# Four graph layers on one core: the projections of the attention layers done two chunks at a time, side by side, with half of the split operands filled by DMA

## The reference

```
L0: h = x @ W (row 0 set to 0); h2 = mask^T summed h; score = h.a1 + h2.a2; out = leaky(score * sum(h))
L1: h = x @ Wh for 4 heads; scores = h h^T; softmax over the masked row; attn @ h + bh, leaky_relu;
    the 4 heads side by side -> z; h2 = z @ Wo; the same attention once more; leaky_relu, layernorm
L2: h = x @ W; e = leaky(h.a_l + (h.a_r)^T, 0.01); masked softmax; attn @ h
L3: the same with slope 0.2 and the other weights
```

## Time and profile before

| | before |
|---|---|
| runs | 6273.06, 6281.87, 6285.5 us (median 6281.87) |
| profiled execution | 6281.5 us, of which the span from the first to the last instruction is 6279.7 us |
| TensorE matmul busy | 5612.5 us, 89% of the span |
| VectorE, ScalarE, GpSimd busy | 4379.2, 3844.2, 1784.7 us |
| mean granted TensorE clock | 0.956 |
| moved by DMA | 55.36 MB |

### The profile page before, as it was taken

How to read it: one execution, slowest core, us unless ns; L and a number is a source line. 1 busy time by engine, 2 the same in 40 slices (tenths; PEclk the granted TensorE clock), 3 DMA queues, 4 the chain that set the end, 5 groups by cost and what they waited for, 6 DMA issues and landing times.

```text
span 6279.7 us, 163342 instructions
## 1 busy us (share of the span) xinstructions
PE 5612.5 (89%) x52064; PEld 4569.8 (73%) x52064; DVE 4379.2 (70%) x7705; ACT 3844.2 (61%) x5701; POOL 1784.7 (28%) x1659
## 2 busy tenths in 40 slices
PE   7679998998989889998989989898899989899866
PEld 4368777886768777786778867787777867788755
DVE  4856567767776677767777677766777677776765
ACT  1046557666576666667576666767576675766665
POOL 0100015014240424205250242404242052402455
PEclk9889999999999999999999999999999999999988
DMA  4200000000000000000000000000000000000000
GB/s 142 59 11 2 2 5 2 2 2 10 4 2 2 2 12 2 2 2 3 11 2 2 2 10 4 2 2 2 12 2 2 2 3 11 2 2 2 8 1 5
DMA packets 98616, 55.36 MB, mean 9 GB/s; under 512 B 88800, under 2 KB 92128, under 8 KB 97760
## 3 DMA queue, kind: packets, MB, share of 16 engines
q1 hardware_dynamic: 59872, 34.45, 2.0%
q10 hardware_dynamic: 37888, 9.97, 0.7%
HBM read 35.49 MB, written 8.91 MB: 7 GB/s over the span
## 4 chain that ended last, share of the span: by engine, by line
PE 69%; issue 9%; DVE 7%; ACT 5%; DVEq 3%; POOLq 1%; POOL 1%; ACTq 0%; DMA 0%; SPq 0%
PE tp L917 22%; PE po L937 20%; PE pss L905 9%; PE pss L906 9%; DVEq L259 3%; DVE rows L1193 2%; PE px L866 2%; DVE pt L1205 2%; PE px L925 2%; ACT pss L1077 1%; ACT rows L1097 1%; PE px L862 1%; POOLq L259 1%; PE px L880 1%; PE px L872 1%
## 5 line engine op out<-in xcount | busy, mean ns | idle before, releaser
L917 PE MATMUL tp<-ident,rows 128*128 128x128 f32 x14336 | 2003.1, 282 | 165.0 <-DVE pt L1205 116.4
L1205 DVE COPY pt<-tp 128x512 f32<-128x512 f32 x2048 | 1339.1, 687 | 1071.8 <-PE tp L917 1060.0
L917 PEld LDWEIGHTS tp<-ident,rows 128*128 128x128 f32 x14336 | 1630.5, 144 | 498.5 <-issue 433.3
L1097 ACT ACTIVATE rows<-rows,nm 128x2048 f32<-128x2048 f32 x896 | 1795.3, 2004 | 287.1 <-DVE nm L1193 278.7
L937 PE MATMUL po<-pt,hn 128*64 128x128 f32 x28672 | 1808.6, 280 | 35.0 <-ACT ot L1058 33.5
L937 PEld LDWEIGHTS po<-pt,hn 128*64 128x64 f32 x28672 | 1593.7, 140 | 194.6 <-issue 194.4
L1050 ACT COPY pt<-tp 128x512 f32<-128x512 f32 x1536 | 840.9, 589 | 722.1 <-PE tp L917 715.6
L748 POOL TENSOR_TENSOR rows<-sr,mask 128x2048 f32<-128x2048 f32 x256 | 1046.8, 4092 | 290.2 <-PE tp L917 282.1
L905 PE MATMUL pss<-ha 128*128 128x512 f32 x2560 | 1072.8, 419 | 15.0 <-issue 12.7
L906 PE MATMUL pss<-ha,hb 128*128 128x512 f32 x2560 | 1018.7, 398 | 0.0
L1193 DVE CUSTOM_DVE_ANT_0 rows<-pss,mask,nm 128x1024 f32<-128x1024 f32 x640 | 821.8, 1284 | 210.4 <-issue 207.6
(11 more groups left out here) (105 smaller groups left out, 3500.8 us busy)
## 6 DMA issues: line engine op xcount, KB each, us to landing
adjb<-in_adj SPq DMA_DIRECT2D x32, 512.0 KB, 4.6
xin<-x SPq DMA_DIRECT2D x34, 128.0 KB, 2.3
xb<-in_x ACTq DMA_DIRECT2D x16, 256.0 KB, 3.3
x<-t ACTq DMA_DIRECT2D x16, 256.0 KB, 2.7
xb<-x SPq DMA_DIRECT2D x8, 512.0 KB, 5.0
out<-xb SPq DMA_DIRECT2D x32, 128.0 KB, 1.9
xtp<-in_xt SPq DMA_DIRECT2D x12, 256.0 KB, 6.9
ab<-in_a ACTq DMA_DIRECT2D x16, 64.0 KB, 3.1
```

The lines of the kernel that those rows point to most:

```text
L917: last = nc.tensor.transpose(tp[q % 2][:, r * P:(r + 1) * P], rows[:, row.slot, jb * P:(jb + 1) * P], ident[:])
L1097: nc.scalar.activation(rows[:, row.slot, :], rows[:, row.slot, :], ACT.Exp, scale=-1.0, bias=nm[:, row.place, 1:2], accum_out=rs[:, row.pl ...
L1205: nc.vector.tensor_copy(pt[:, CH * q:CH * (q + 1), row.k % SLOTS, :], tp[q % 2][:].rearrange("p (j n) -> p j n", n=P)).then_inc(pt_dve, 1)
```

## The change

`proj` and `hn` take two chunks at once (a group g of 1024 nodes, 2 groups per batch and unit). The weights hold the 64 columns once. The projection runs in 4 column blocks of 128, each as two matmuls that write the upper and the lower partition half of `px`: the even chunk above, the odd chunk below. For GAT2 each has two matmuls to accumulate. ScalarE copies the whole bank once to a new tile `hc` (exact), which frees `px`; it then makes two rounded copies out of `hc` and VectorE two subtractions, with both operands in SBUF. They fill one partition half of `ha` and `hb` for each chunk. The other half is the same data, and SP fills it with four DMAs per group from SBUF to SBUF (`mirror_halves`); TensorE waits for them (`halves_in`) at the first row of a unit. `hn` is 4 full transposes of `hc` and one ScalarE copy for both chunks. In `h`, the two small operations on left and right terms go from VectorE to ScalarE. The tasks have new steps: head 1 is projected in the rows of head 0 (steps 22 to 27) instead of in those of ADD1 (36 to 43), and the `xt`, `h` and `r` of ADD2 go from steps 80 to 87.5 to steps 53 to 83.

```diff
-    tasks += [("before", name, 0, c) for c in range(NC) for name in ("proj", "hn")]
+    tasks += [("before", name, 0, g) for g in range(2) for name in ("proj", "hn")]
     for u in range(H - 1):
-        for c in range(NC):
-            tasks += [(NB * u + 3 + 3 * c, "proj", u + 1, c), (NB * u + 4 + 3 * c, "hn", u + 1, c)]
+        for g in range(2):
+            tasks += [(NB * u + 4 + 5 * g, "proj", u + 1, g), (NB * u + 5 + 5 * g, "hn", u + 1, g)]
...
-    tasks += [(end - 4, "z0", GAT2, 0), (end - 3, "z1", GAT2, 0), (end - 1, "z0", GAT2, 1), (end - 0.5, "z1", GAT2, 1)]
-    tasks += [(end, "proj", GAT2, 0), (end + 3, "z0", GAT2, 2), (end + 3.5, "z1", GAT2, 2), (end + 4, "hn", GAT2, 0)]
-    tasks += [(end + n, name, GAT2, c) for c, n in ((1, 5), (2, 6)) for name in ("proj", "hn")]
-    tasks += [(end + GAP - 1, name, GAT2, 3) for name in ("z0", "z1", "proj", "hn")]
+    tasks += [(end - 4, "z0", GAT2, 0), (end - 3, "z1", GAT2, 0), (end - 1, "z0", GAT2, 1), (end, "z1", GAT2, 1)]
+    tasks += [(end + 1, "proj", GAT2, 0), (end + 3, "z0", GAT2, 2), (end + 4, "z1", GAT2, 2), (end + 5, "hn", GAT2, 0)]
+    tasks += [(end + GAP - 1, name, GAT2, 3) for name in ("z0", "z1")]
+    tasks += [(end + GAP - 1, name, GAT2, 1) for name in ("proj", "hn")]
...
-        xn, proj, hn = ((8, 9, 9.5), (10, 10.5, 11), (11.5, 12, 13), (13.5, 14, 15))[c]
-        tasks += [(xn, "xn", 0, c), (proj, "proj", 0, c), (hn, "hn", 0, c)]
+        tasks += [((8, 9, 10, 11.5)[c], "xn", 0, c)]
         tasks += [(10 + n, "la", GAT2, c), (11 + n, "lb", GAT2, c), (13 + n, "lc", GAT2, c), (14 + n, "ld", GAT2, c)]
         tasks += [(15.5 + n, "xt", ADD1, c), (16 + n, "h", ADD1, c), (17 + n, "r", ADD1, c)]
-        tasks += [(36 + 2 * c, "proj", 1, c), (37 + 2 * c, "hn", 1, c)]
-        tasks += [(50 + 3 * c, "proj", 2, c), (51 + 3 * c, "hn", 2, c)]
-        tasks += [(68 + 3 * c, "proj", 3, c), (69 + 3 * c, "hn", 3, c)]
         for unit in (ADD1, ADD2):
             end = at(order, unit, n + CH - 1)
             tasks += [(end + 7, "ra", unit, c), (end + 8, "rb", unit, c)]
-        tasks += [(80 + 2 * c, "xt", ADD2, c), (81 + 2 * c, "h", ADD2, c), (81.5 + 2 * c, "r", ADD2, c)]
-    end = [at(order, H - 1, CH * c + CH - 1) for c in range(NC)]
-    last = end[NC - 1]
-    tasks += [(end[0] + 8, "z0", GAT2, 0), (end[0] + 8.5, "z1", GAT2, 0)]
-    tasks += [(end[1] + 8, "z0", GAT2, 1), (end[1] + 8.5, "z1", GAT2, 1), (last + 1, "proj", GAT2, 0)]
-    tasks += [(last + 4, "z0", GAT2, 2), (last + 4.5, "z1", GAT2, 2), (last + 5, "hn", GAT2, 0)]
-    tasks += [(last + 6, "proj", GAT2, 1), (last + 6.5, "hn", GAT2, 1)]
-    tasks += [(last + 8, "proj", GAT2, 2), (last + 8.5, "hn", GAT2, 2)]
-    tasks += [(last + 10, "z0", GAT2, 3), (last + 10.5, "z1", GAT2, 3)]
-    tasks += [(last + 12, "proj", GAT2, 3), (last + 12.5, "hn", GAT2, 3)]
+        xt = (53, 59, 71, 81)[c]
+        tasks += [(xt, "xt", ADD2, c), (xt + 1, "h", ADD2, c), (xt + 2, "r", ADD2, c)]
+    for unit, times in ((0, (9.5, 11, 12, 13)), (1, (22, 23, 26, 27)), (2, (51, 52, 57, 58)), (3, (69, 70, 75, 76))):
+        for g in range(2):
+            tasks += [(times[2 * g], "proj", unit, g), (times[2 * g + 1], "hn", unit, g)]
+    last = at(order, H - 1, NB - 1)
+    tasks += [(last - 4, "z0", GAT2, 0), (last - 3, "z1", GAT2, 0), (last, "z0", GAT2, 1), (last + 1, "z1", GAT2, 1)]
+    tasks += [(last + 2, "proj", GAT2, 0), (last + 4, "z0", GAT2, 2), (last + 5, "hn", GAT2, 0)]
+    tasks += [(last + 6, "z1", GAT2, 2), (last + 8, "z0", GAT2, 3), (last + 9, "z1", GAT2, 3)]
+    tasks += [(last + 10, "proj", GAT2, 1), (last + 11, "hn", GAT2, 1)]
...
+            def mirror_halves(unit, g):
+                ha_u, hb_u = ha[PROJ[unit]], hb[PROJ[unit]]
+                low_c.n += 1
+                wait(low_c)
+                for chunk, own, other in ((2 * g, slice(0, D), slice(D, P)), (2 * g + 1, slice(D, P), slice(0, D))):
+                    cols = slice(chunk * BANK, (chunk + 1) * BANK)
+                    sp.dma_start(hb_u[other, cols].bitcast(F32), ha_u[own, cols].bitcast(F32)).then_inc(halves_in, 16)
+                    sp.dma_start(ha_u[other, cols].bitcast(F32), hb_u[own, cols].bitcast(F32)).then_inc(halves_in, 16)
...
+            for unit in range(H + 1):
+                for g in range(2):
+                    mirror_halves(unit, g)
...
+                enter_loop(counts, b)
                 for c in range(2, NC + 2):
-                    src = x1[bass.ds(b + 1 + c // NC, 1)].rearrange("o (k p) d -> p (o k) d", p=P)
-                    stand_alone_wait(sp, xn_psum, b * NC + NC + c - 1, gates)
-                    sp.dma_start(xin[:, c % 2], src[:, c % NC * CH:(c % NC + 1) * CH, :])\
-                      .then_inc(xin_in[c % 2], 16)
+                    load_chunk(x1[bass.ds(b + 1 + c // NC, 1)].rearrange("o (k p) d -> p (o k) d", p=P), c)
+                    if c == 3:
+                        mirror_halves(0, 0)
+                mirror_halves(0, 1)
+                for unit in range(1, H + 1):
+                    for g in range(2):
+                        mirror_halves(unit, g)
...
-                    if unit == GAT2:
-                        wait(zt_c)
-                        for k in range(2):
-                            last = nc.tensor.matmul(px[:], wo[:, k, :], zt[:, c % 2, k, :],
-                                                    start=(k == 0), stop=(k == 1))
-                    else:
-                        wait(xn_c)
-                        last = nc.tensor.matmul(px[:], wh[:, unit, :], xt[:, cols], start=True, stop=True)
+                    wait(zt_c if unit == GAT2 else xn_c)
+                    for q in range(CH):
+                        own = slice(q * P, (q + 1) * P)
+                        for k in range(2 if unit == GAT2 else 1):
+                            for side in range(2):
+                                if unit == GAT2:
+                                    weights, moving = wo[:, k, :], zt[:, side, k, own]
+                                else:
+                                    first = (2 * c + side) * BANK + q * P
+                                    weights, moving = wh[:, unit, :], xt[:, first:first + P]
+                                last = nc.tensor.matmul(px[side * D:(side + 1) * D, own], weights, moving,
+                                                        start=(k == 0), stop=(k == 1 or unit != GAT2))
                     last.then_inc(proj_psum, 1)
-                    px_used(h2_c)
+                    px_used(hc_c)
+                    halves_c.n += 64
                 elif name == "hn":
                     px_free()
+                    wait(hc_c)
                     for q in range(CH):
-                        last = nc.tensor.transpose(px[:, q * D:(q + 1) * D], hf[:, q * P:(q + 1) * P],
-                                                   ident[D:P, D:P])
+                        block = slice(q * P, (q + 1) * P)
+                        last = nc.tensor.transpose(px[:, block], hc[:, block], ident[:])
                     last.then_inc(hn_psum, 1)
                     px_used(hn_c)
                 elif name == "h":
...
                         last = nc.tensor.matmul(px[:, q * (D + 2):(q + 1) * (D + 2)], xc[:, q * P:(q + 1) * P],
                                                 wl[D:P, unit - ADD1, :], start=True, stop=True)
                     last.then_inc(hn_psum, 1)
-                    px_used(lr_c)
-                    hn_c.n += 1
+                    lr_c.n += 1
+                    px_used(hn_c)
...
                 if row.t == 0:
-                    wait(h2_c)
+                    wait(halves_c)
...
-                    i = PROJ[unit]
+                    i, top, bottom = PROJ[unit], slice(2 * c * BANK, (2 * c + 1) * BANK), \
+                        slice((2 * c + 1) * BANK, (2 * c + 2) * BANK)
+                    if low_c.n or low_c.batch is not None:
+                        wait(low_c)
+                    low_c.n += 1
                     next_of(proj_c)
-                    nc.scalar.copy(ha[i][0:D, cols], px[0:D, :])
-                    nc.scalar.copy(hb[i][D:P, cols], px[D:P, :])
-                    nc.scalar.copy(hf, px[D:P, :]).then_inc(h1_ready, 1)
+                    nc.scalar.copy(hc[:], px[:]).then_inc(hc_ready, 1)
+                    next_of(hc_c)
+                    nc.scalar.copy(ha[i][0:D, top], hc[0:D, :])
+                    nc.scalar.copy(hb[i][D:P, bottom], hc[D:P, :]).then_inc(high_ready, 1)
                 elif name == "hn":
                     next_of(hn_c)
-                    nc.scalar.copy(hn[hn_of(unit)][:, blocks, :],
-                                   px[:, 0:CH * D].rearrange("p (k d) -> p k d", d=D)).then_inc(hn_ready, 1)
+                    both = hn[hn_of(unit)][:, 2 * CH * c:2 * CH * (c + 1), :]
+                    nc.scalar.copy(both.rearrange("p (s k) d -> p k s d", s=2),
```

(73 more changed lines are left out.)

15 lines of the change are left out of this document (7 added, 8 removed).

## The result

| | before | after |
|---|---|---|
| median (lowest to highest) of 4 runs each | 6283.68 us (6273.06 to 6287.03) | 5970.62 us (5969.27 to 5974.46) |
| ratio, 95% interval | | 0.9506 (0.9489 to 0.9522) |
| profiled execution, its span | 6281.5, 6279.7 us | 5974.5, 5972.7 us |
| mean granted clock | 0.956 | 0.967 |

The account below looks back on a forecast made before the run. TensorE was taken as the bound overall, ScalarE in ADD rows. Savings of 40.3 us a batch, 282 in seven batches, plus 39 in the prologue made 321; 6281.5 - 321 = 5960 us, range 5865 to 6070.

Parts of the forecast that it names:

- Heads 2 and 3: Loop windows of these two heads' projections: 16.2 us a batch now, 6.4 after, 9.8 us a batch saved.
- head 1: Its projection leaves the ADD rows for GAT rows: of 15.2 us 1.5 stays, 3.2 is added elsewhere; 10.5 us a batch saved.
- head 0: Loop window of 9 GAT rows with the loop's turn: excess 22.5 us falls to 14.0, 8.5 us a batch saved.
- prologue: Before the loop: three heads save 15 us, the start 12 and the gap before GAT2 12, 39 in all.
- the 73.5 named as a sign: Sign that the forecast holds: windows of heads 2 and 3 near 73.5 us.
- GAT2: Loop stretch of one GAT and 13 ADD rows: excess 32.7 us falls to 21.2, 11.5 us a batch saved.
- the lock: VectorE's two-SBUF-operand subtractions and GpSimd block each other: 0 to 4.1 us each, taken as 1 us per GAT2 group.
- (a): Rival: the projection's 64-row column tiles don't run side by side, a group costs 2.1 us; 6065 us, chance 0.08.
- (b): Rival: VectorE and GpSimd blocking decides, 14 loop groups at 8.2 us instead of 1.0; 6060 us, chance 0.08.
- (c): Rival: only TensorE's work on the changed lines goes, 188 us, and other waits fill the rest; 6093 us, chance 0.07.
- (d): Rival: more goes, also some 13 us a batch of remaining waits or low clock, 91 us; 5870 us, chance 0.12.
- (e): Rival: the DMAed halves land late, so each unit waits at its first row; slower, about 6740 us, chance 0.02.

## Why the prediction was right

**The bound and the bases.** Where no task of the change stands nothing moved: steps 1 to 7 take 38.7 us before and 38.6 after (mean of the batches, of which the first follows the prologue and takes 32), steps 32 to 35 20.8 in both. Reading each stretch against its own base row is what made the terms come out.

**Heads 2 and 3, head 1, head 0, prologue.** Each term is within 2 us of its measured value. The four rows of the loop were forecast at -28.8 us a batch and gave -31.4, the prologue at -39 and gave -42.2. The head group costs 1.09 us on TensorE where 0.95 was priced, and without a lead the transfers cost 6.15 us a unit (12.3 / 2) where 4.3 was, both small. The window of head 2 takes 75.3 us and not the 73.5 named as a sign, since two chunks of ADD2's `xt`, `h` and `r` now stand in it; over steps 48 to 94, where they stood before as well, the saving is as forecast. Head 1's two groups in the GAT rows cost 2.2 us, not 3.2. The mechanism is shown from three sides: column tiles 49 us when given back, the bank 44, head 1's place 59 (a part of it the collision at step 43). These are prices inside the new kernel, one at a time, and no split of the 313 us. They sum to 152; the rest, with the halved copies, subtractions and transposes, has no run of its own, nor have the operations of `h` moved to ScalarE. What I had not seen is that some of the heads' saving, 2.9 us a batch, is to be had by the old tasks' place alone.

**The step that was mis-sized** is GAT2: "2 projections of 4.4 (2 to 3 us of TensorE at either clock, 1.74 of ScalarE)". I wrote that the wait for ScalarE's copy stays, and then priced TensorE's and ScalarE's own work only. Measured, a step with a projection is 11.46 and 10.15 us long, 6.3 and 4.9 over the row: 2.4 us a batch above the two 4.4. Another 1.6 us is the choice of the window: the 106.0 us of one batch stood for a mean of 104.4. Together that is 4.0 of the 4.3 us a batch that were missing. The other terms of the stretch fit only in their sum: the steps of the two `hn` cost 0.6 us where 2.4 was priced and the subtractions paid nothing for the lock (2.0), while steps 102, 107 and 108, for which I had no term, cost 4.1. Moving the projections to even steps removes their wait and this length with it, though four transpositions of outputs and both `hn` moved too, so the wait is the likely cause and not the only one that the run allows. The saving was forecast 30 us too large over the loop for this stretch. Against it the other loop terms gave 7 x 2.6 = 18 us more than forecast, so the total came nearer than the terms did, which is luck. Steps 109 to 112 lost 1.5 us a batch for which I had no term. They get it back when the projections move (22.4 us) and also when the norms move (20.9), so which of the two costs it is open.

**The rivals.** (a) fell by 1.09 against 1.58 us. (b), the lock, by the subtractions themselves, in the kernel after (min/median/max ns):

```profile
L1193 DVE TENSOR_TENSOR hb<-hc,ha x80: 672/683/686, 334.1 to 5543.4; 64x512 fp32r<-64x512 f32 x80
```

```profile
L1194 DVE TENSOR_TENSOR ha<-hc,hb x80: 687/689/1012, 334.8 to 5544.1; 64x512 fp32r<-64x512 f32 x80
```

None of 160 sat through a mask addition of 4 us; the longest is 0.32 us over the median. My 1 us a group was thus too much: in this trace no subtraction overlaps a mask addition, and at step 97 GpSimd stands waiting 2.63 us for the transposes just then. The Trainium skill, "SBUF — State Buffer", section "Who interferes with whom", states that a VectorE instruction with two SBUF inputs and a GpSimd instruction that reads SBUF shut each other out. The trace agrees where the two meet: the norm instruction of 0.43 us takes 4.29 us at step 107, and 4.33 us in the run with head 1 in the ADD rows. (c), 6093, would need the waits for `px` to be replaced; they went. (d), 5870, is 23 us under the lowest median of any run here: a part of the slack it spoke of exists, but it takes moved tasks, which this change does not bring. (e) by the transfers made twice.
